# Attention's values, prediction and gram move from the third layer's second column to one visit with attn_out at the end of the second layer, on one Trainium2 core

## The reference

```python
h = layernorm(x) * (1 + ca) + sa
# attention on h: values v = h @ Ww.T, unit vectors rk = h / |h| per head, wk = rk one token back
A = inv(I + strict(wk wk^T * L))             # per chunk of 64, from the "gram" of unit vectors
v_new = A @ v - (A @ wk) @ S                 # S: the state carried from chunk to chunk
o = (rk * g) @ S + strict(rk wk^T * L) @ v_new
S = gamma^64 * S + (wk * g')^T @ v_new
x = x + ga * (h + o @ Wr.T)                  # "attn_out" is the product with Wr
h = layernorm(x) * (1 + cb) + sb
f = silu(h @ w1 * s1) * (h @ w2 * s2)        # "l1": 256 -> 1024, two matrices
f = gelu(f @ h1 * t1)                        # "l2": 1024 -> 1024
f = gelu(f @ h2 * t2)                        # "l3": 1024 -> 1024
x = x + gb * (f @ w3 * s3)                   # "y":  1024 -> 256
```

## Time and profile before

| | before |
|---|---|
| median of 3 runs | 1699.47 us (1698.02 to 1701.67) |
| the profiled execution | 1700.03 us, of which the profiled span is 1698.1 us |
| PE busy | 1677.2 us, 99% of the span |
| DVE, ACT, POOL busy | 67%, 59%, 35% |
| granted TensorE clock | 0.991 of 2.4 GHz on average |

### The profile page before, as it was taken

The page is one execution under the profiler, slowest core; times in us unless marked ns, Lnnn a source line. Parts: engine busy times, 40 slices in busy tenths (PEclk is TensorE's granted clock), DMA queues, the critical chain, the costliest instruction groups (busy, mean ns, idle before and its releaser), DMA issues.

```text
span 1698.1 us, 59356 instructions
## 1 busy us (share of the span) xinstructions
PE 1677.2 (99%) x24310; PEld 1619.7 (95%) x24310; DVE 1144.6 (67%) x3223; ACT 1004.8 (59%) x2389; POOL 596.6 (35%) x694
## 2 busy tenths in 40 slices
PE   8899999999999999999999999999999999999998
PEld 7798999999999999999999999999999999999998
DVE  5777667776666776766776766776766776766432
ACT  4764665556656556666556665555665555665554
POOL 3544333343333243433243333234333234333101
PEclk8899999999999999999999999999999999999999
DMA  8202223332223332222332222322222332222110
GB/s 279 89 21 41 49 47 61 55 55 43 50 48 56 55 58 42 49 48 56 56 57 44 49 49 53 61 52 44 51 50 49 61 54 44 52 49 42 21 20 8
DMA packets 396492, 92.13 MB, mean 54 GB/s; under 512 B 368372, under 2 KB 388472, under 8 KB 396216
## 3 DMA queue, kind: packets, MB, share of 16 engines
q1 hardware_dynamic: 394224, 85.87, 25.8%
q10 hardware_dynamic: 1992, 2.38, 0.5%
HBM read 45.07 MB, written 30.94 MB: 45 GB/s over the span
## 4 chain that ended last, share of the span: by engine, by line
PE 94%; DVE 2%; POOL 1%; DMA 1%; issue 1%; ACT 1%; SPq 0%; ACTq 0%; DVEq 0%; POOLq 0%
PE mlp L1249 66%; PE mlp L1323 7%; PE solo L1249 3%; PE solo L1407 3%; PE duo L1545 3%; PE solo L1222 2%; PE duo L1215 1%; PE solo L1232 1%; PE duo L1432 1%; PE duo L1210 1%; PE duo L1534 1%; PE duo L1419 1%; PE duo L1536 1%; PE duo L1455 1%; POOL act_lo L699 1%
## 5 line engine op out<-in xcount | busy, mean ns | idle before, releaser
L1249 PE MATMUL mlp<-act_hi,w_hi 128*128 128x256 f32 x4096 | 975.1, 283 | 1.2 <-POOL act_lo L699 0.6
L1249 PE MATMUL mlp<-act_lo,w_hi 128*128 128x256 f32 x4096 | 954.5, 278 | 0.0
L1249 PEld LDWEIGHTS mlp<-act_hi,w_hi 128*128 128x128 f32 x4096 | 771.2, 188 | 12.0 <-POOL act_lo L699 1.4
L1249 PEld LDWEIGHTS mlp<-act_lo,w_hi 128*128 128x128 f32 x4096 | 771.8, 188 | 0.8
L858 ACT ACTIVATE full<-mlp,scale_sb 128x256 f32<-128x256 f32 x512 | 242.6, 474 | 444.1 <-PE mlp L1249 441.8
L961 DVE TENSOR_TENSOR act_lo<-full,act_hi 128x256 fp32r<-128x256 f32 x512 | 260.3, 508 | 276.4 <-ACT act_hi L859 274.2
L699 POOL TENSOR_TENSOR act_lo<-full,act_hi 128x256 fp32r<-128x256 f32 x256 | 186.9, 736 | 484.5 <-ACT act_hi L848 484.5
L859 ACT ACTIVATE act_hi<-mlp,scale_sb 128x256 fp32r<-128x256 f32 x512 | 240.1, 469 | 0.0
L1249 PE MATMUL mlp<-xh,w_hi 128*128 128x256 f32 x768 | 180.5, 278 | 1.3 <-DVE full L1093 1.3
L1249 PE MATMUL mlp<-xl,w_hi 128*128 128x256 f32 x768 | 179.7, 277 | 0.0
L1093 DVE SCALAR_TENSOR_TENSOR full<-mlp,scale_sb,gate 128x256 f32<-128x256 f32 x192 | 92.7, 484 | 87.4 <-ACT gate L843 83.3
(11 more groups left out here) (198 smaller groups left out, 2734.7 us busy)
## 6 DMA issues: line engine op xcount, KB each, us to landing
w_raw<-in_wts SPq DMA_DIRECT2D x22, 512.0 KB, 5.2
kg<-r SPq DMA_DIRECT2D x64, 126.0 KB
xin<-in_x SPq DMA_DIRECT2D x62, 128.0 KB, 2.8
out_y<-y SPq DMA_DIRECT2D x62, 128.0 KB, 2.5
x_squares<-o_state SPq DMA_DIRECT2D x30, 256.0 KB, 3.2
vn<-x_squares SPq DMA_DIRECT2D x120, 64.0 KB, 2.2
h_squares<-near SPq DMA_DIRECT2D x28, 256.0 KB, 3.3
hT<-h_squares SPq DMA_DIRECT2D x112, 64.0 KB, 2.2
```

Source lines behind the costliest of these rows:

```text
L1249: mm = pe.matmul(dst, *general_ops, start=is_first and i == 0, stop=is_last and i == 1)
```

## The change

Five edits, all of the order:

1. values, pred and gram for chunk n+2 (no longer n+1) stand behind l2 7, in one visit with attn_out, which itself moves from behind l2 6 to behind l2 7. The visit behind l3 1 is gone. attn_out writes `solo[1]` instead of `duo[1][:, 0]`, so that gram can follow at once.
2. norm and flip 0 move from behind l2 0 to behind l1 7; square from l2 2 to l2 0; length, unit and flip 1 from l2 3 and l2 4 to l2 2. ACT's rows moves from l3 0 to l2 7.
3. POOL's far (the mask for the next lead) moves from l1 7 to l2 5, and PE waits for it in l1 5 instead of in lead. POOL's decay of the state waits for norm (`h_ready`), and its near and cross masks wait for norm2 (`xn2_ready`).
4. A table `fourth` is walked in step 3 alone: it has values, pred and gram twice, for chunk 4 behind l3 1 as before, and for chunk 5 behind l2 7. The loop then covers steps 4 to 27.
5. Three warm-up matmul groups before the first step run as 128-column pieces instead of 512-column ones, as many columns in all.

```diff
-    mixed = listed([("norm2", 0, 0), ("turn", 0, 0)], late + layers[:2 * HK], {
-        ("l3", 0): [("rows", 0, 1)],
-        ("l3", 1): [("values", 0, 1), ("pred", 0, 0), ("gram", 0, 1), ("intra", 0, 1), ("u", 0, 0), ("fs", 0, 1)],
+    between = {
+        ("l3", 1): [("intra", 0, 1), ("u", 0, 0), ("fs", 0, 1)],
         ("l3", 2): [("fs", 1, 1)],
...
-        ("l1", 7): [("stats", 0, 2), ("lead", 0, 0), ("far", 0, 1)],
-        ("l2", 0): [("old", 0, 0), ("norm", 0, 2), ("flip", 0, 2)],
+        ("l1", 7): [("stats", 0, 2), ("lead", 0, 0), ("norm", 0, 2), ("flip", 0, 2)],
+        ("l2", 0): [("old", 0, 0), ("square", 0, 2)],
         ("l2", 1): [("keys", 0, 0)],
-        ("l2", 2): [("join", 0, 0), ("wide", 0, 1), ("square", 0, 2)],
-        ("l2", 3): [("length", 0, 2)],
-        ("l2", 4): [("n", 3, 1), ("unit", 0, 2), ("state", 0, 0), ("flip", 1, 2)],
-        ("l2", 5): [("residual", 0, 2), ("rg", 0, 1)],
-        ("l2", 6): [("attn_out", 0, 0)],
+        ("l2", 2): [("join", 0, 0), ("wide", 0, 1), ("length", 0, 2), ("unit", 0, 2), ("flip", 1, 2)],
+        ("l2", 4): [("n", 3, 1), ("state", 0, 0)],
+        ("l2", 5): [("residual", 0, 2), ("rg", 0, 1), ("far", 0, 1)],
+        ("l2", 7): [("rows", 0, 2), ("attn_out", 0, 0), ("values", 0, 2), ("pred", 0, 1), ("gram", 0, 2)],
...
+    def attended(items):
+        return solo[1][:] if items in steady else duo[1][:, 0, :]
...
                     if name == "gram":
+                        if items is mixed or items is fourth and a == 5:
+                            pool.wait_ge(xn2_ready, n + 1)
...
                         pool.wait_ge(inter_full, a)
+                        if items in steady and (not isinstance(n, int) or n + 2 < STEPS):
+                            pool.wait_ge(h_ready, n + 3)
...
+                        if k == 5 and items in steady and (not isinstance(n, int) or n < STEPS):
+                            pe.wait_ge(far_ready, n + 1)
+                            pe.wait_ge(diag_ready, n + 1)
...
                     if name == "attn_out":
...
+                        if items in steady:
+                            pe.wait_ge(diag_ready, begun(n, items))
                         pe.wait_ge(oT_ready, now)
```

More of the change, by code:

```diff
@@ L400, in run @@
         step(2, 2, third)
+        step(3, 3, fourth)
         passes = (STEPS - 5) // PASS
@@ L403, in run @@
             for j in range(PASS):
-                step(PASS * i + 3 + j, (3 + j) % (2 * BASES), mixed)
-        for n in range(3 + PASS * passes, STEPS + 2):
+                step(PASS * i + 4 + j, (4 + j) % (2 * BASES), mixed)
+        for n in range(4 + PASS * passes, STEPS + 2):
             step(n, n % (2 * BASES), mixed)
@@ L573, in step @@
                 whole = not isinstance(n, int)
-                if items is mixed and (whole or n <= STEPS):
+                if items in steady and (whole or n <= STEPS):
                     move_normed(n)
@@ L579, in step @@
                         load_last(n - 1)
-                    if items is mixed and (whole or n + 1 < STEPS):
+                    if items in steady and (whole or n + 1 < STEPS):
                         attention(n + 1, (g + 1) % 2)
@@ L595, in step @@
                     attention(n + 1, (g + 1) % 2)
-                if items in (third, mixed) and (whole or n + 2 < STEPS):
+                if items in (third, *steady) and (whole or n + 2 < STEPS):
                     move_blocks(n + 2)
@@ L675, in part @@
                         after(pool, x1_ready, a - 2)
-                        if items is mixed or items is third and a == n + 2:
+                        if items in steady or items is third and a == n + 2:
                             pool.wait_ge(r_turned, a - 3)
@@ L804, in part @@
                         ins.then_inc(wide_ready, 1)
-                    if name == "n" and k == 3 and items is mixed:
+                    if name == "n" and k == 3 and items in steady:
                         act.wait_ge(rest_full, now)
@@ L810, in part @@
                         ins.then_inc(diag_ready, 1)
-                    if name == "n" and k == 3 and items is not mixed:
+                    if name == "n" and k == 3 and items not in steady:
                         block_diagonal(a)
@@ L823, in part @@
                     if name == "ln2":
-                        if k == 0 and items is mixed:
+                        if k == 0 and items in steady:
                             act.wait_ge(x_rows_in, READS * n - 2 * READS)
-                        if k == 0 and items is not mixed:
+                        if k == 0 and items not in steady:
                             act.wait_ge(h2T_full, n)
@@ L988, in part @@
                         dve.transpose(by_square(h_blocks), h[:].rearrange("p b (k c n) -> p c (b k) n", k=KT, n=SQ)).then_inc(h_turned, 1)
-                    if name == "turn" and items is mixed:
+                    if name == "turn" and items in steady:
                         dve.wait_ge(xn2_ready, n)
@@ L1285, in layer @@
                                 weights_in(m, unit[name, k])
-                            if items is mixed and name == "l2" and k == 2 and (not isinstance(n, int) or n + 1 < STEPS):
+                            if items in steady and name == "l2" and k == 2 and (not isinstance(n, int) or n + 1 < STEPS):
                                 pe.wait_ge(inv_moved, 32 * n - 64)
@@ L1330, in part @@
                     now, p = a + 1, phase % 2
-                    paired = name == "l3" and k < 2 and items is mixed and not general
+                    paired = name == "l3" and k < 2 and items in steady and not general
                     if name in ("l1", "l2", "l3") and not paired:
@@ L1359, in part @@
                     if name == "warm_end":
-                        warm(k, duo[1][:, 1, :])
+                        warm(k, duo[1][:, 1, :], P)
                     if name == "flag" and k == 0:
@@ L1392, in part @@
                             pe.wait_ge(tables_ready, 1)
-                        if items is not mixed:
+                        if items not in steady:
                             pe.wait_ge(hT_ready, now)
@@ L1460, in part @@
                                 mm = first_term(m, c, c)
-                        for e, q, c, i in quarters if k == 2 or k == 3 and items is not mixed else ():
+                        for e, q, c, i in quarters if k == 2 or k == 3 and items not in steady else ():
                             rows, m = quarter(c, i), e * NP + q
@@ L1494, in part @@
                             pe.wait_ge(inv_ready, n + 2)
-                        pe.wait_ge(far_ready, now)
-                        pe.wait_ge(diag_ready, now)
+                        if name == "solve":
+                            pe.wait_ge(far_ready, now)
+                            pe.wait_ge(diag_ready, now)
                         if items is alone:
@@ L1544, in part @@
                             for hp in range(H // 2):
-                                mm = pe.matmul(duo[1][:, 0, b * D:(b + 1) * D], o_state[:, b * (H // 2) + hp, :], wr_turned[:, hp, :],
+                                mm = pe.matmul(attended(items)[:, b * D:(b + 1) * D], o_state[:, b * (H // 2) + hp, :], wr_turned[:, hp, :],
                                                start=hp == 0, stop=hp == H // 2 - 1)
                         mm.then_inc(ao_full, 1)
-                    if name == "turn" and items is not mixed:
+                    if name == "turn" and items not in steady:
                         if items is opening:
```

48 lines of the change are left out of this document (27 added, 21 removed).

## The result

| | before | after |
|---|---|---|
| median | 1700.26 us (10 runs, 1698.02 to 1701.67) | 1703.78 us (10 runs, 1700.36 to 1706.02) |
| ratio | | 1.0021, 95% interval 1.0011 to 1.0030 |
| the profiled execution | 1700.03 us, span 1698.1 | 1701.3 us, span 1699.5 |
| granted TensorE clock | 0.991 | 0.994 |

A forecast was written before the change was run, and what follows sets the result against it. The prediction took PE, busy 99% of the span, as the bound. Terms -0.8 + 1.3 + 0 + 0.5 = +1.0 us on the profiled 1700.03, 0.56 above the median of 1699.47, gave 1700.5 us; range 1692 to 1706.

The forecast's parts named there:

- One visit less: On PE around attn_out: going in and out of one visit is saved, -0.03 us a step, -0.8 us in all.
- rival D: PE stops in the long visit for rT: 0.2 us a step, +6 us; chance 0.12 together with Rival C.
- The uncovered pause: At l3 2 PE waits for ACT on l3 0, flipping the pace each time: +0.045 us a step, +1.3 us.
- a sign that the prediction gave for being wrong: In PE's chain, the l3 pieces of 96 matmuls being all of one kind instead of alternating 11.5 and 11.1 us.
- The share of the slow pace: PE's matmuls over a step: fast and slow steps alternate, 152 slow matmuls a step before and after, 0 us.
- The rules: On PE, attn_out, values, join and pauses flip the pace, state keeps it, lead takes l3's; slow costs 4.4 ns a matmul.
- Rival A: Merged visit and join leave the pace, which settles fast: 48 slow matmuls a step, -12 us, 1688; chance 0.25 beyond 0.2%.
- rival B: Pace settles slow: 1703.0 us if the merged visit keeps it, 1713 without join's flip; chance 0.15.
- norm and its followers sooner: DVE and POOL rows made sooner: hT and rT still come in time, PE's cover is enough, 0 us.
- x_squares: Read before ACT's ln2 behind l3 5: still in time in the steady part, late once in step 32, +0.5 us.
- Rival C: x_squares late at ACT's ln2, holding up l3 6 and 7: 0.3 us a step, +8 us, 1709; chance 0.12 with rival D.
- the rest: far, POOL's masks, flag and warm-up groups, `fourth`: all 0, with 1 us either way for the start.

The follow-up runs named there:

- e8: The changed kernel with attn_out back in a visit of its own behind l2 6; 1719.67 us, ratio 1.0132 to the kernel before.
- e1: The changed kernel run again, word for word; 1710.38 us, ratio 1.0066 to the kernel before.
- e9: The kernel before with step 3 written out and the loop making one pass, steps 4 to 15; 1698.25 us, ratio 0.9991.
- e6: The kernel before with only the second edit, the norm's rows sooner, far not moved; 1713.22 us, ratio 1.0090.
- e7: The changed kernel with the hardware loop making one pass, steps 4 to 15, the rest written out; 1695.55 us, ratio 0.9982 to the kernel before.
- e3: The changed kernel without the hardware loop, steps from 4 on written out; 1698.97 us, ratio 0.9999 to the kernel before.
- e10: e7 with l3 0 and l3 1 one after the other instead of interleaved; 1700.44 us, ratio 1.0007 to the kernel before.

## Why the prediction was right or wrong

The forecast was 1700.5 us and no difference within 0.2%; it came out at 1703.8, 0.21% slower, inside the range. By the line that the prediction drew itself, slower from 1702.9 on, it is just on the slower side. The sum of +1.0 us on the profiled execution stands against a measured +1.3, but that is luck: two of its terms were wrong, by about -5 and +4 us, and with 1.4 us at the start and 1.7 us of small stops they came out near it.

**One visit less, -0.8 us.** The visit stands as forecast: four pieces without a wait between them, 924.18 to 928.72 = 4.54 us, against "some 4.4 us". The 0.03 us a step can't be told apart from pace in any trace. What e8 adds is that the merged visit is worth 0.51 us a step more than two, by the cover for rT; the prediction names this cover and was right that it suffices (rival D did not happen).

**The uncovered pause, +1.3 us.** Right in size, and there in every step. Timeline of PE in after, a step with a slow l3 0, and one with a fast:

```profile
932.53 0.30 PE L1261 MATMUL mlp<-act_hi,w_hi 128*128 128x256 f32 x1
932.66 0.28 PE L1261 MATMUL mlp<-act_lo,w_hi 128*128 128x256 f32 x1
```

```profile
982.94 0.34 PE L1261 MATMUL mlp<-act_hi,w_hi 128*128 128x256 f32 x1
983.12 0.28 PE L1261 MATMUL mlp<-act_lo,w_hi 128*128 128x256 f32 x1
```

0.13 and 0.18 us, against the 0.14 and 0.19 of the earlier trace rows. "Each time the pace flips" was right for e1 and wrong here: behind it the pace is fast in both. With that a sign that the prediction gave for being wrong came true: the 96 matmuls from l3 2 on are all of one kind.

**The share of the slow pace, 0.** This is the first step that failed. I took 152 slow matmuls a step before and after. By the chain above a pair of steps has 32 (l3 0 and 1) + 16 (y) + 64 (l1), and 16 + 64: 96 a step. 56 fewer at 4.4 ns are -0.25 us; with +0.045 and -0.03 the step should be 0.235 shorter. It is 0.185 shorter (101.35 to 100.98 a pair), -5.0 us over 27 steps, where the sum had 0 for the pace and +0.4 for pause and visit. The rules broke at three places: join does not flip, l3 2 is fast behind either pause, and l1, fast before, is slow. Rival A's mechanism (join without a flip) was there in part, rival B's in e1. That a pace "holds until the next visit or pause" stands in the pieces shown. Which pace follows is not a property of the visit: before and e9 have the same visits and 50.54 against 50.81 us steps, after and e1 are one program. What sets it was not found.

**norm and its followers sooner, 0.** Right for the kernel as changed, wrong as reasoned: I looked at when hT and rT are ready, and not at what GpSimd does beside the h rows. In e6, where far has not moved, PE waits 0.36 us a step for it on average, and a step is 0.14 us longer.

**x_squares, 0 in the steady part and +0.5 in step 32.** Right in place, too large in size: in all of after ScalarE waits for it once, 0.2 us, in step 32. Rival C did not happen.

**The loop's end, no term at all.** This is the second failure, and the one that made the kernel slower. The prediction never names the loop's shift: the step more in front of it stands under "the rest" as "`fourth` adds no matmul", at 0. That instructions are moved during the run was to be seen on the page of before:

```profile
q8 instruction: 197, 3.23, 0.8%
```

The loop's end costs 3.55 us in the profiled execution (104.53 against 100.98), 4.1 and 5.4 us in the two repeats, and 0 where the loop ends with step 15 after one pass (e7) or isn't there (e3).

**The sum again,** between the two profiled executions: start +1.4 us (lead of step 3 at 195.58 against 194.15); -5.0 by pace and visit; +3.8 at the loop's end (3.55 over two clean steps, where before lies 0.24 under two of its own); +1.7 in other steps (after 2.7 over clean ones, up to 0.65 each, before 1.0). That is +0.5 over 27 steps. The last step and the tail give -0.1. Together +1.8 to the last matmul, +1.4 in the span, +1.3 us in the time. The medians differ by 3.5; the part above 1.3 was not in the profiled execution. The start's 1.4 us was allowed for as 1 us either way, and comes and goes: lead of step 3 is at 194.04 in e10 and at 197.56 in e1.

## What to carry over

Moving a hardware loop by one step is a change of its own: look in the trace for waits on nothing ("issue") in the steps behind the loop's end and its turn, look whether an `instruction` packet ends 1.3 to 1.4 us ahead of where they end, and try the end at other places or without the loop before judging what is inside. When VectorE's rows are moved, read which GpSimd rows they come to lie beside. And when a difference of 0.2% comes from how fast equal matmuls follow each other, run the same kernel again first, on the same chip and on another: here a repeat moved the ratio from 1.0021 to 1.0066.

## What was not expected of the hardware

- Behind the hardware loop's end PE stood still for 1.4 to 1.7 us and VectorE for 2.5 to 2.6, between instructions that need nothing new, in all six traces in which the loop ends with step 27, PE's own stop in l3 1 in the five of them with the changed order; in the changed kernel with the end at step 15 after one pass (e7, e10), or without the loop (e3), not at all. Stops of this kind end 1.25 to 1.46 us behind the end of a packet of instructions.
- Matmuls of one shape (128x256) stand 117.5 or 113.1 ns apart at a granted clock of 1.00, for whole stretches, and the same program had another pattern of the two in another run (after and e1).
- A pause of 0.01 to 0.07 us on PE stands where the pace of the 96 matmuls behind it is settled: fast in all but one step of four traces, slow in 25 of 27 steps of a fifth.
- Two VectorE instructions of 128x256 took 2.13 us beside GpSimd's, 0.87 without them.
